# Centring ahead of the first layer and scaling by rstd after its products, for half of the tokens

## The chip, the cores and the metric

The kernel runs on one core of a Trainium2 chip. A core has a matrix engine (TensorE, "PE" in the profile), a vector engine (VectorE, DVE), a scalar engine (ScalarE, ACT), GpSimd (POOL), and SyncE (SP), which here only issues DMA transfers. Each engine runs its own list of instructions in order; they meet at semaphores. The metric is the device time of one execution in microseconds (us).

## What is computed

There are 1024 tokens of 256 features. Two layers, each behind a layer norm and added to its input; cut from the reference:

```
def _layernorm(x, axis=-1, eps=1e-05):
    m = jnp.mean(x, axis=axis, keepdims=True)
    v = jnp.var(x, axis=axis, keepdims=True)
    return (x - m) / jnp.sqrt(v + eps)
...
    # first layer: 4 experts, one per token, all three weights are the same ctx[e]
    for e in range(E):
        g = jax.nn.silu(jnp.einsum('bsd,fd->bsf', hidden_states, Wg[e]))
        u = jnp.einsum('bsd,fd->bsf', hidden_states, Wu[e])
        y = jnp.einsum('bsf,df->bsd', g * u, Wd[e])
        out = jnp.where((expert_ids == e)[..., None], y, out)
...
x = x + _L0_xattn_ref(_layernorm(x, axis=-1), itok_BxS_13_99985, ctx_2048, ctx_2048, ctx_2048)
x = x + _L0_ffn_ref(_layernorm(x, axis=-1), L0_ffn_router_w, ...)
```

In the first layer g and u use the same matrix, so the kernel computes one product z = xn ctx[e], picks for each token the one of its expert, and forms silu(z) z. The second layer has 16 routed experts of width 96 (4 per token) and a shared one. Because (x - m) ctx[e] rstd is the same as ((x - m) rstd) ctx[e], the scale by rstd, a number for each token, can be put before or after the product.

## The kernel before

Features lie on partitions (two blocks of 128, k = 0 and 1) and tokens along the rows, in two halves (h) of 512. A float32 value is split into a high part in the matrix engine's format (`_hi`) and the rest (`_lo`), and a product takes three matmuls: hi·hi, hi·lo and lo·hi.

**The norm.** x arrives by DMA with tokens on partitions, in tiles of 128 tokens; half 0 is tiles 0 to 3. DVE takes statistics of each tile (`tile_stats`, `layer_norm_vars`), POOL raises the variance to the power -0.5 (`rstd_of`), DVE makes `shift` = -mean rstd, and then DVE (tiles 0 and 2, by `BY_VECTOR`) and ACT (tiles 1 and 3) write the normed tile `xn` (`layer_norm_apply`, `apply_norm`). For half 0 this is done in two pairs of tiles. PE turns each `xn` tile with two transposes (`norm_transposes`) into banks 4 and 5; ACT copies them to `xn_hi` (`x_high`), DVE subtracts to get `xn_lo` (`x_low`).

**The mixes.** The first layer is eight calls `mix(n)`: mixes 0 and 1 are the first product of half 0 (output features 0 to 127 and 128 to 255), 2 and 3 those of half 1, 4 to 7 the second product. A mix has 4 experts with 6 matmuls of 128x512 each. The product of each expert goes into the next bank of a ring of six (banks 0 to 3, 6, 7). ACT copies expert 0 to `prod` (`first_z`), DVE copies experts 1 to 3 over it where a mask `beyond` says so (`pick`). ACT makes the silu (`silu_z`), DVE the product and its two parts (`hidden_1`), which mixes 4 to 7 read. A bank is free for PE again when its copy is done (`wait_ring_read`). Half 1's transposes stand inside mix 1, behind its expert 1.

**Weights.** They come in 15 pieces through 4 stage slots. For each, ACT writes the high part (`high_part`) and POOL the low part (`low_part`); pieces 0 to 3 are the experts' ctx matrices. SP issues all transfers in one hand-written order on one queue, and piece n waits until the parts of piece n - 4 are made.

**Before the first data.** PE runs 20 matmuls on a zeroed tile (`WARM_UP`), writing bank 7, then waits for the identity matrix (`consts_in`) and the first `xn` tile. The second layer's matmuls stand behind mix 7; the order on PE is fixed from start to end.

Of the kernel before, what the change touches and what calls it, by code (L numbers as in the profile page):

```python
# [19 lines left out]
F32 = mybir.dt.float32  # L20
# [4 lines left out]
ALU = mybir.AluOpType  # L25
# [25 lines left out]
WARM_UP = 20  # L51
# [11 lines left out]
SPREADS = 4  # L63
RING = HALVES * KC
# [14 lines left out]
def build(nc, x_d, xt_d, ids_d, ctx_d, bias_d, gu_d, wd0_d, wd_d, consts_d, out_d):  # L79
# [4 lines left out]
    with ExitStack() as ctx:  # L84
# [7 lines left out]
        x = sb("x", [P, HALVES * TT, D])  # L92
# [17 lines left out]
        shift = sb("shift", [P, NORMS, TT])  # L110
        power = sb("power", [P, TT])
# [42 lines left out]
        ids_in, xt_in, bias_in, consts_in = sem("ids_in"), sem("xt_in"), sem("bias_in"), sem("consts_in")  # L154
# [6 lines left out]
        dstep = sem("dstep")  # L161
# [22 lines left out]
        side_order = [("n1", 0, 0, 4), ("n1", 0, 1, 5), ("n1", 1, 0, 4), ("n1", 1, 1, 5),  # L184
# [12 lines left out]
        def wait_side_read(eng, b, n):  # L197
# [5 lines left out]
            if what in ("n1", "n2"):  # L203
                count = (HALVES * KC if what == "n2" else 0) + h * KC + k + 1
                eng.wait_ge(xhi_done, count)
                eng.wait_ge(xlo_done, count)
            elif what == "x1":
# [142 lines left out]
        def _(sp):  # L350
# [14 lines left out]
            sp.dma_start(x[:, TT:], x_d[:, TT:]).then_inc(x_in[2], 16)  # L365
            sp.dma_start(ids[:], ids_d.partition_broadcast(P)).then_inc(ids_in, 16)
            sp.dma_start(xt[:], xt_d).then_inc(xt_in, 16)
# [39 lines left out]
        def _(pool):  # L407
# [36 lines left out]
            rstd_of(2, 4)  # L444
            low_part(early_pieces)
            low_part(early_pieces + 1)
            rstd_of(3, 5)
# [4 lines left out]
        def _(act):  # L452
# [19 lines left out]
            def apply_norm(n, tiles=range(TT)):  # L472

                act.wait_ge(shifted, n + 2 if n > 0 or tiles[0] > 0 else 1)
                if n > 0:
                    what, hh = [("n1", 0), ("n1", 1), ("n2", 0)][n - 1]
                    act.wait_ge(side_done, side_at[what, hh, 1] + 1)
                for t in tiles:
# [4 lines left out]
            def silu_z(n):  # L483
                act.wait_ge(z_picked, (n + 1) * (E1 - 1))
# [68 lines left out]
            x_high("n1", 1, 0)  # L553
            x_high("n1", 1, 1)
            silu_z(1)
# [41 lines left out]
        def _(dve):  # L597
# [15 lines left out]
            def layer_norm_vars(n, tiles=range(TT)):  # L613
# [5 lines left out]
                s = slice(tiles[0], tiles[-1] + 1)  # L619
                nc.vector.tensor_scalar(vareps[:, n, s], meanvar[:, n, s, 1], EPS, None, ALU.add).then_inc(varied, 1)  # L620

            def layer_norm_apply(n, tiles=range(TT)):

                dve.wait_ge(powered, n + 2 if n > 0 or tiles[0] > 0 else 1)
                s = slice(tiles[0], tiles[-1] + 1)
                nc.vector.scalar_tensor_tensor(out=shift[:, n, s], in0=meanvar[:, n, s, 0], scalar=-1.0, in1=rstd[:, n, s],
                                               op0=ALU.mult, op1=ALU.mult).then_inc(shifted, 1)
                if n > 0:

                    what, hh = [("n1", 0), ("n1", 1), ("n2", 0)][n - 1]  # L630
                    dve.wait_ge(side_done, side_at[what, hh, 1] + 1)
                for t in tiles:
# [4 lines left out]
            def x_low(what, h, k):  # L637
                n = (HALVES * KC if what == "n2" else 0) + h * KC + k
                dve.wait_ge(xhi_done, n + 1)
# [187 lines left out]
            for n, tiles in enumerate((range(TT // 2), range(TT // 2, TT))):  # L827
                dve.wait_ge(x_in[n], 16)
                for t in tiles:
                    tile_stats(0, t)  # L830
                layer_norm_vars(0, tiles)
            for n, tiles in enumerate((range(TT // 2), range(TT // 2, TT))):
                layer_norm_apply(0, tiles)
            x_low("n1", 0, 0)
            x_low("n1", 0, 1)
            dve.wait_ge(x_in[2], 16)
# [304 lines left out]
```

## Time and profile before

| | us |
|---|---|
| median of 3 runs | 175.72 |
| lowest, highest | 175.63, 175.94 |
| the profiled execution | 175.69 |
| its span in the profile | 173.6 |

The page gives for this execution, over the span of 173.6 us: PE busy 168.2, DVE 117.6, ACT 68.1, POOL 40.3. The span begins when the engines start and ends with their last instruction; 2.1 us of the execution's time lie outside it. A busy time counts overlapping instructions once, and says nothing on whether anyone waits for them: for this the chain of waits and the order of time are read.

### The profile page before, as it was taken

To read this page: it belongs to the slowest core of one execution; us is meant where nothing else is said; L and a number is where in the kernel's file an instruction comes from. 1 tells how busy PE (TensorE), PEld (TensorE's weight loads), DVE (VectorE), ACT (ScalarE), POOL (GpSimd) and SP (SyncE) were. 2 spreads that over 40 slices of the span, in tenths; PEclk is the share of its full clock that TensorE was granted. 3 is DMA by queue.
4 is the path that set the end of the run, shared out by engine and by line. 5 is a ranking of instruction groups with operands and counts; after the bars stand their busy time and mean duration, and the time that the engine had idled before them with its cause. 6 is when DMAs were issued, how large, how long until landed. Compare 5 with 4: busy or idle time off the path is not lost.

```text
span 173.6 us, 2253 instructions
## 1 busy us (share of the span) xinstructions
PE 168.2 (97%) x738; PEld 131.9 (76%) x738; DVE 117.6 (68%) x267; ACT 68.1 (39%) x108; POOL 40.3 (23%) x41
## 2 busy tenths in 40 slices
PE   6989999999999999999999999999999999999992
PEld 2558888888888878888888788888878888878881
DVE  0779897885588697787688649995874544444452
ACT  2462431343115965724654582222332222222320
POOL 5593011674220006439385000000000000000000
PEclk9999999999999999999999999999999999999999
DMA  4999004065400006951111100004454221100003
GB/s 139 283 414 337 11 0 123 0 178 184 121 0 4 0 4 144 265 144 62 60 60 60 60 0 4 0 0 125 125 194 140 81 66 65 66 5 0 0 0 121
DMA packets 7451, 15.82 MB, mean 91 GB/s; under 512 B 1296, under 2 KB 1904, under 8 KB 7312
## 3 DMA queue, kind: packets, MB, share of 16 engines
q1 hardware_dynamic: 7440, 15.68, 28.5%
q8 instruction: 6, 0.10, 0.2%
q14 instruction: 5, 0.04, 0.1%
HBM read 14.56 MB, written 1.11 MB: 90 GB/s over the span
## 4 chain that ended last, share of the span: by engine, by line
PE 89%; DVE 3%; ACT 3%; DMA 2%; issue 1%; DVEq 0%; ACTq 0%
PE bank L955 24%; PE bank L1038 13%; PE bank L1037 13%; PE bank L1036 13%; PE bank L1056 7%; PE bank L1059 7%; PE bank L1057 7%; DMA x<-x_d 2%; PE bank L917 2%; PE bank L933 1%; DVE stats L611 1%; PE bank L1033 1%; PE bank L1032 1%; ACT L490 1%; ACT xn L480 1%
## 5 line engine op out<-in xcount | busy, mean ns | idle before, releaser
L1038 PE MATMUL bank<-xn_lo,gu_hi 128*128 128x512 f32 (+1 forms) x104 | 41.1, 395 | 0.0
L1036 PE MATMUL bank<-xn_hi,gu_lo 128*128 128x512 f32 x96 | 38.1, 397 | 0.0
L1037 PE MATMUL bank<-xn_hi,gu_hi 128*128 128x512 f32 x96 | 38.0, 395 | 0.0
L538 ACT ACTIVATE h_hi<-hid 128x512 fp32r<-128x512 f32 (+1 forms) x26 | 16.4, 632 | 44.4 <-DVE hid L813 44.4
L818 DVE TENSOR_TENSOR h_lo<-hid,h_hi 128x512 fp32r<-128x512 f32 (+1 forms) x26 | 21.6, 830 | 14.1 <-ACT h_hi L538 14.0
L1038 PEld LDWEIGHTS bank<-xn_lo,gu_hi 128*128 128x128 f32 (+1 forms) x104 | 19.4, 187 | 4.9
L528 ACT ACTIVATE act_sb<-bank 128x512 f32<-128x512 f32 (+1 forms) x26 | 15.4, 592 | 16.7 <-PE bank L1038 16.6
L423 POOL TENSOR_TENSOR gu_lo<-stage,gu_hi 128x512 fp32r<-128x512 f32 x12 | 16.8, 1417 | 21.4 <-ACT gu_hi L456 21.3
L1037 PEld LDWEIGHTS bank<-xn_hi,gu_hi 128*128 128x128 f32 x96 | 18.0, 188 | 4.3
L1036 PEld LDWEIGHTS bank<-xn_hi,gu_lo 128*128 128x128 f32 x96 | 18.0, 188 | 4.2
L662 DVE COPY_PREDICATED prod<-beyond,bank 128x512 f32<-128x512 uint8 x24 | 17.8, 740 | 4.9 <-PE bank L955 3.8
L1056 PE MATMUL bank<-h_hi,wd_lo 128*128 128x512 f32 (+1 forms) x52 | 20.8, 399 | 0.0
L1059 PE MATMUL bank<-h_lo,wd_hi 128*128 128x512 f32 (+1 forms) x52 | 20.6, 395 | 0.0
L1057 PE MATMUL bank<-h_hi,wd_hi 128*128 128x512 f32 (+1 forms) x52 | 20.6, 395 | 0.0
L813 DVE TENSOR_TENSOR hid<-prod,bank 128x512 f32<-128x512 f32 x24 | 16.5, 687 | 1.7
L800 DVE TENSOR_TENSOR prod<-act_sb,ids 128x512 f32<-128x512 f32 x10 | 7.6, 764 | 10.2 <-ACT act_sb L528 8.9
L800 DVE TENSOR_TENSOR prod<-act_sb,x 128x512 f32<-128x512 f32 x12 | 9.3, 778 | 7.1 <-ACT act_sb L528 7.1
L955 PE MATMUL bank<-xn_hi,ctx_hi 128*128 128x512 f32 x32 | 12.8, 400 | 0.7 <-ACT xn_hi L463 0.7
L955 PE MATMUL bank<-h_hi,ctx_hi 128*128 128x512 f32 x32 | 12.9, 403 | 0.0
L955 PE MATMUL bank<-xn_lo,ctx_hi 128*128 128x512 f32 x32 | 12.8, 399 | 0.0
L955 PE MATMUL bank<-xn_hi,ctx_lo 128*128 128x512 f32 x32 | 12.7, 396 | 0.0
L955 PE MATMUL bank<-h_lo,ctx_hi 128*128 128x512 f32 x32 | 12.7, 395 | 0.0
(104 smaller groups left out, 224.1 us busy)
## 6 DMA issues: line engine op xcount, KB each, us to landing
stage<-gu_d SPq DMA_DIRECT2D x6, 512.0 KB, 3.5
stage<-wd_d SPq DMA_DIRECT2D x3, 512.0 KB, 5.1
x<-comb_d SPq DMA_DIRECT2D x8, 192.0 KB, 2.8
ids<-comb_d SPq DMA_DIRECT2D x7, 192.0 KB, 2.7
stage<-ctx_d SPq DMA_DIRECT2D x4, 256.0 KB, 5.3
xt<-xt_d SPq DMA_DIRECT2D x1, 1024.0 KB, 9.5
x<-comb_d SPq DMA_DIRECT2D x8, 128.0 KB, 2.8
ids<-comb_d SPq DMA_DIRECT2D x6, 128.0 KB, 3.3
```

The costliest lines, as they stand in the source:

```text
L423: ins = nc.gpsimd.tensor_tensor(lo[:, s], st[:, s], hi[:, s].bitcast(F32), ALU.subtract)
L662: nc.vector.copy_predicated(prod[:, n % 2], beyond[:, e - 1, h * HALF:(h + 1) * HALF], ring_bank("z", n, e)[:]).then_inc(z_picked, 1)
L800: nc.vector.tensor_tensor(prod[:, g % 2], act_sb[:, g % 2], rows, ALU.mult).then_inc(prod_done, 1)
L813: nc.vector.tensor_tensor(hid[0:w, g % 2], src, up_bank(g)[0:w, :], ALU.mult).then_inc(hid_done, 1)
L818: nc.vector.tensor_tensor(h_lo[0:w, slot[g]], hid[0:w, g % 2], h_hi[0:w, slot[g]].bitcast(F32), ALU.subtract).then_inc(hlo_done, 1)
L955: return nc.tensor.matmul(ring_bank("z", n, e)[:], (ctx_hi, ctx_lo)[a][:, e, k, f], parts[k][b], start=start, stop=stop)
L1036: nc.tensor.matmul(out[:], gu_lo[:, cols], xn_hi[:, h, k], start=(k == 0), stop=False)
L1037: nc.tensor.matmul(out[:], gu_hi[:, cols], xn_hi[:, h, k], start=False, stop=False)
L1038: ins = nc.tensor.matmul(out[0:rows, :], gu_hi[:, wide], xn_lo[:, h, k], start=False, stop=(k == KC - 1))
L1056: nc.tensor.matmul(acc[k][:], wd_lo[0:w, c, cols], hi, start=(c == 0), stop=False)
L1057: nc.tensor.matmul(acc[k][:], wd_hi[0:w, c, cols], hi, start=False, stop=False)
L1059: ins = nc.tensor.matmul(acc[k][:], wd_hi[0:w, c, cols], lo, start=False, stop=(c == ITEMS - 1))
```

## The change

Half 0 is only centred before its products: `xn` becomes x - mean, with no rstd. `centre(t)` does this tile by tile: DVE takes mean and difference of tiles 0 and 2; ACT, by itself, of tiles 1 and 3, with a sum over the row (`accum_out` of a copy scaled by -1/256) and a second pass that adds it. The variances of half 0 are still needed: DVE takes the missing statistics of tiles 1 and 3 afterwards, POOL computes `rstd_of(0)` after the four low parts of ctx, PE turns its 128x4 numbers into 4 rows behind mix 0 (`rstd_transpose`), ACT copies them, SP writes them to DRAM and reads them back to all 128 partitions (`rstd_all`, which lies in the still unused end of `wd_lo`), and DVE multiplies `prod` of mixes 0 and 1 by them (`scale`), behind the picks and ahead of silu. Half 1 and the second layer's norms are as before.

Around this: the identity and x tiles 0 and 1 come in one transfer of 324 KB (`first_d`) in the place of 256 KB and a later one of 68 KB; DVE makes `xn_hi` of k = 1 of half 0 in ACT's place; the first mix waits for both `xn_hi` blocks and takes its six matmuls for each expert in the order hi·hi twice, lo·hi twice, hi·lo twice; there are 8 matmuls of 512 columns ahead and 8 of 256 columns between and behind the transposes in the place of 20 of 512; on DVE `hidden_1` of mixes 0 and 1 and the masks of half 1 stand later; on SP the transfers of xt, bias and pieces 4 and up stand behind the waits for the rstd rows.

```diff
-WARM_UP = 20
+WARM_UP = 8
...
-        side_order = [("n1", 0, 0, 4), ("n1", 0, 1, 5), ("n1", 1, 0, 4), ("n1", 1, 1, 5),
+        side_order = [("n1", 0, 0, 4), ("n1", 0, 1, 5), ("rstd", 0, 0, 4), ("n1", 1, 0, 4), ("n1", 1, 1, 5),
...
-            sp.dma_start(x[:, 0:TT // 2], x_d[:, 0:TT // 2]).then_inc(x_in[0], 16)
-            sp.dma_start(x[:, TT // 2:TT], x_d[:, TT // 2:TT]).then_inc(x_in[1], 16)
+            sp.dma_start(first[:, 0:FIRST + PAIR], first_d).then_inc(x_in[0], 16)
+            sp.dma_start(first[:, FIRST + PAIR:FIRST + 2 * PAIR], x_d[:, 0:PAIR]).then_inc(x_in[1], 16)
             load_piece(0)
-            sp.dma_start(consts_sb[:], consts_d).then_inc(consts_in, 16)
...
             sp.dma_start(ids[:], ids_d.partition_broadcast(P)).then_inc(ids_in, 16)
+            sp.wait_ge(rstd_turned, 1)
+            sp.dma_start(rstd_d, rstd_rows[:]).then_inc(rstd_out, 16)
+            sp.wait_ge(rstd_out, 16)
+            sp.dma_start(rstd_all, rstd_d.rearrange("t c -> (t c)").partition_broadcast(P)).then_inc(rstd_in, 16)
             sp.dma_start(xt[:], xt_d).then_inc(xt_in, 16)
...
-            rstd_of(0, 1, slice(0, TT // 2))
-            rstd_of(0, 2, slice(TT // 2, TT))
             for n in range(E1):
                 low_part(n)
-            rstd_of(1, 3)
-            pool.wait_ge(consts_in, 16)
+            rstd_of(0)
+            rstd_of(1)
+            pool.wait_ge(x_in[0], 16)
...
+            def centre(t):
+
+                act.wait_ge(x_in[t // (TT // 2)], 16)
+                nc.scalar.activation(xn[:, t], x[:, t], ACT.Copy, scale=-1.0 / D,
+                                     accum_out=minus_mean[:, t:t + 1]).then_inc(astep, 1)
+                act.wait_ge(astep, t // 2 + 1)
+                nc.scalar.activation(xn[:, t], x[:, t], ACT.Identity, bias=minus_mean[:, t:t + 1]).then_inc(normed_a, 1)
+
+            def turn_rstd():
+
+                act.wait_ge(side_done, side_at["rstd", 0, 0] + 1)
+                nc.scalar.activation(rstd_rows[:], side_bank("rstd", 0, 0)[0:TT, 0:P], ACT.Copy).then_inc(rstd_turned, 1)
...
             def silu_z(n):
-                act.wait_ge(z_picked, (n + 1) * (E1 - 1))
+                if mixes[n][1] == 0:
+                    act.wait_ge(z_scaled, n + 1)
+                else:
+                    act.wait_ge(z_picked, (n + 1) * (E1 - 1))
...
-            apply_norm(0, range(TT // 2))
+            centre(1)
+            centre(3)
             high_part(0)
-            apply_norm(0, range(TT // 2, TT))
+            x_high("n1", 0, 0)
             high_part(1)
-            x_high("n1", 0, 0)
-            x_high("n1", 0, 1)
             high_part(2)
             high_part(3)
             first_z(0)
+            turn_rstd()
             apply_norm(1)
-            silu_z(0)
             first_z(1)
             x_high("n1", 1, 0)
             x_high("n1", 1, 1)
+            silu_z(0)
             silu_z(1)
...
+            def centre(t):
+
+                dve.wait_ge(x_in[t // (TT // 2)], 16)
+                tile_stats(0, t)
+                dve.wait_ge(dstep, steps[0])
+                step(nc.vector.bn_aggr(meanvar[:, 0, t], stats[:, t]))
+                dve.wait_ge(dstep, steps[0])
+                nc.vector.tensor_scalar(xn[:, t], x[:, t], meanvar[:, 0, t, 0:1], None, ALU.subtract).then_inc(normed_v, 1)
+
+            def scale(n):
+
+                dve.wait_ge(rstd_in, 16)
+                dve.wait_ge(z_picked, (n + 1) * (E1 - 1))
+                nc.vector.tensor_tensor(prod[:, n % 2], prod[:, n % 2], rstd_all, ALU.mult).then_inc(z_scaled, 1)
...
+            centre(0)
+            centre(2)
+            dve.wait_ge(side_done, side_at["n1", 0, 1] + 1)
+            nc.vector.tensor_scalar(xn_hi[:, 0, 1], side_bank("n1", 0, 1)[:], 1.0, None, ALU.mult).then_inc(xhi_done, 1)
             x_low("n1", 0, 0)
             x_low("n1", 0, 1)
+            tile_stats(0, 1)
+            tile_stats(0, 3)
+            layer_norm_vars(0, (1, 3))
...
             pick(0, masked[0], [2, 3])
-            hidden_1(0)
             x_low("n1", 1, 0)
             x_low("n1", 1, 1)
+            scale(0)
             pick(1, masked[0])
+            scale(1)
+            hidden_1(0)
+            hidden_1(1)
             masked.append(thresholds(1))
-            hidden_1(1)
             pick(2, masked[1])
...
+                    if n == 0:
+                        for k in range(KC):
+                            operands(k, False)
+                            term(e, k, 0, 0, start=(k == 0))
+                        for k in range(KC):
+                            operands(k, True)
+                            term(e, k, 0, 1)
+                        pe.wait_ge(w_lo, e + 1)
+                        for k in range(KC):
+                            ins = term(e, k, 1, 0, stop=(k == KC - 1))
...
-            for _ in range(WARM_UP):
-                nc.tensor.matmul(bank[7][:], warm[:, 0:P], warm[:], start=True, stop=True)
-            pe.wait_ge(consts_in, 16)
-            norm_transposes("n1", 0, 0)
+            keep_warm(WARM_UP)
+            pe.wait_ge(x_in[0], 16)
+            norm_transposes("n1", 0, 0, (0, 2, 2, 1))
+            keep_warm(3, HALF // 2)
             mix(0)
+            rstd_transpose()
```

On PE, at the start of the program before (`bank` is a PSUM bank; in brackets the semaphores waited for):

```order
L1068 MATMUL bank<-warm 128x512 [waits warm_set]
L1068 MATMUL bank<-warm 128x512 x19
L917 MATMUL bank<-consts_sb,xn 128x128 [waits normed_v,consts_in]
L917 MATMUL bank<-consts_sb,xn 128x128
L917 MATMUL bank<-consts_sb,xn 128x128 [waits normed_a]
...
L955 MATMUL bank<-xn_hi,ctx_hi 128x512 [waits xhi_done,w_hi]
L955 MATMUL bank<-xn_hi,ctx_lo 128x512 [waits w_lo]
L955 MATMUL bank<-xn_lo,ctx_hi 128x512 [waits xlo_done]
```

The same place after:

```order
L953 MATMUL bank<-warm 128x512 x7
L963 MATMUL bank<-first,xn 128x128 [waits normed_v,x_in0]
L963 MATMUL bank<-first,xn 128x128
L953 MATMUL bank<-warm 128x256 x2
L963 MATMUL bank<-first,xn 128x128 [waits normed_a]
...
L953 MATMUL bank<-warm 128x256 x3
L1007 MATMUL bank<-xn_hi,ctx_hi 128x512 [waits xhi_done,w_hi]
L1007 MATMUL bank<-xn_hi,ctx_hi 128x512 [waits xhi_done]
L1007 MATMUL bank<-xn_lo,ctx_hi 128x512 [waits xlo_done] x2
L1007 MATMUL bank<-xn_hi,ctx_lo 128x512 [waits w_lo]
```

The zero matmuls are fewer and stand between the transposes, and in the first mix the matmul that needs POOL's low part of the weights went from second to fifth place.

On DVE, from the picks of mix 0 on, before:

```order
L634 TENSOR_SCALAR xn<-x,meanvar,rstd 128x256 x2
L662 COPY_PREDICATED prod<-beyond,bank 128x512 x2
L670 TENSOR_TENSOR hid<-act_sb,prod 128x512
L672 TENSOR_SCALAR h_hi<-hid 128x512
L674 TENSOR_TENSOR h_lo<-hid,h_hi 128x512
L641 TENSOR_TENSOR xn_lo<-bank,xn_hi 128x512 x2
L662 COPY_PREDICATED prod<-beyond,bank 128x512 x3
L648 TENSOR_SCALAR beyond<-ids 128x512 x3
```

and after:

```order
L679 TENSOR_TENSOR xn_lo<-bank,xn_hi 128x512 [waits side_done,xhi_done] x2
L661 TENSOR_TENSOR prod<-prod,wd_lo 128x512 [waits z_picked,rstd_in]
L700 COPY_PREDICATED prod<-beyond,bank 128x512 [waits z_done,dstep,z_first]
L700 COPY_PREDICATED prod<-beyond,bank 128x512 [waits z_picked,z_done] x2
L661 TENSOR_TENSOR prod<-prod,wd_lo 128x512 [waits z_picked,rstd_in]
L708 TENSOR_TENSOR hid<-act_sb,prod 128x512 [waits z_silu]
L710 TENSOR_SCALAR h_hi<-hid 128x512 [waits dstep]
L712 TENSOR_TENSOR h_lo<-hid,h_hi 128x512 [waits h1_high]
```

Two multiplications by the rstd rows (`wd_lo` is where they lie) came in, the first of them waits for a transfer, and the hidden values of mix 0 are made after the picks of mix 1 where they were made before them.

On SP, the queue of transfers after, from the tokens' ids on; before, the row of xt follows the row of ids at once:

```order
L375 DMA ids<-ids_d 128x1024
L377 DMA rstd_d<-rstd_rows 4x128 [waits rstd_turned]
L379 DMA wd_lo<-rstd_d 128x512 [waits rstd_out]
L380 DMA xt<-xt_d 128x2048
L381 DMA bias<-bias_d 128x16
L367 DMA stage<-gu_d 128x448 [waits w_lo,w_hi]
```

Two transfers and two waits came in, and xt, bias and all pieces from the fifth on are queued behind them.

## Rows read from the trace of the kernel before

**Rows 1.** The page: busy time and share by engine; TensorE's granted clock; chain.

```profile
PE 168.2 (97%) x738; PEld 131.9 (76%) x738; DVE 117.6 (68%) x267; ACT 68.1 (39%) x108; POOL 40.3 (23%) x41
PEclk9999999999999999999999999999999999999999
PE 89%; DVE 3%; ACT 3%; DMA 2%; issue 1%; DVEq 0%; ACTq 0%
```

**Rows 2.** The chain that ended last: start us, duration us, what.

```profile
0.74 3.59 DMA x<-x_d
4.35 0.77 DVE stats L611 x2
5.14 0.26 DVE meanvar L617 x2
...
6.83 0.60 ACT xn L480
...
7.95 0.56 ACT xn L480
...
9.03 0.51 ACT xn_hi L463
9.67 8.84 PE bank L955 x36
18.50 0.87 PE bank L917 x8
19.38 28.00 PE bank L955 x120
```

**Rows 3.** The waits of PE: who for whom, us in total, times, longest.

```profile
PE bank L955 <- ACT xn_hi L463: 0.7, 1, 0.7
```

**Rows 4.** Order of time, PE and its weight loads: start us, us, instruction.

```profile
1.31 6.78 PE L1068 MATMUL bank<-warm 128*128 128x512 bf16 x20 [1.31 <-POOL warm L408]
...
5.56 0.15 PEld L1068 LDWEIGHTS bank<-warm 128*128 128x128 bf16 x1 [0.28 <-issue]
...
5.98 1.62 PEld L1068 LDWEIGHTS bank<-warm 128*128 128x128 bf16 x8 [0.27 <-issue]
...
11.34 0.40 PE L955 MATMUL bank<-xn_hi,ctx_hi 128*128 128x512 f32 x1
```

**Rows 5.** Order of time on DVE.

```profile
6.71 0.41 DVE L634 TENSOR_SCALAR xn<-x,meanvar,rstd 128x256 f32<-128x256 f32 x1
...
9.55 1.29 DVE L641 TENSOR_TENSOR xn_lo<-bank,xn_hi 128x512 fp32r<-128x512 f32 x2 [1.36 <-ACT xn_hi L463]
...
17.90 0.69 DVE L670 TENSOR_TENSOR hid<-act_sb,prod 128x512 f32<-128x512 f32 x1 [0.70 <-ACT act_sb L487]
...
21.14 2.42 DVE L662 COPY_PREDICATED prod<-beyond,bank 128x512 f32<-128x512 uint8 x3
...
25.63 1.53 DVE L674 TENSOR_TENSOR h_lo<-hid,h_hi 128x512 fp32r<-128x512 f32 x1
27.08 2.40 DVE L662 COPY_PREDICATED prod<-beyond,bank 128x512 f32<-128x512 uint8 x3
```

**Rows 6.** Order of time on POOL, up to the rstd of half 1.

```profile
8.03 5.12 POOL L419 TENSOR_TENSOR ctx_lo<-stage,ctx_hi 128x512 fp32r<-128x512 f32 x4 [0.35 <-ACT ctx_hi L456]
...
13.25 1.11 POOL L429 TENSOR_TENSOR rstd<-vareps,power 128x4 f32<-128x4 f32 x1
```

**Rows 7.** DMA issues: count, KB each, median us to landing.

```profile
x<-x_d SPq DMA_DIRECT2D x2, 256.0 KB, 3.8
...
comb_d<-comb_row SPq DMA_DIRECT2D x2, 32.0 KB, 1.6
```

**Rows 8.** Stretch 3.00 to 4.35: busy by engine, PEclk, DMA share, GB/s.

```profile
3.00:4.35 1.35, 1.35 (x5) 0.52 (x4) 0.00 (x0) 0.00 (x0) 0.00 (x0) 1.00 0.85 254
```

**Rows 9.** Transfers to and from comb_d, 46 of them, all stages.

```profile
DMA to landing us min/median/max: 1.5/2.8/5.3
```

**Rows 10.** A small ACT instruction of the second layer.

```profile
58.71 0.26 ACT L495 ACTIVATE scores<-logit 128x64 f32<-128x64 f32 x1
```

More of the change, by code:

```diff
@@ L63 @@
 SPREADS = 4
+FIRST = P + GROUPS
+PAIR = TT // 2 * D
 RING = HALVES * KC
@@ L203, in wait_side_read @@
             if what in ("n1", "n2"):
-                count = (HALVES * KC if what == "n2" else 0) + h * KC + k + 1
+                count = (HALVES * KC if what == "n2" else 0) + h * KC + (KC if what == "n1" and h == 0 else k + 1)
                 eng.wait_ge(xhi_done, count)
                 eng.wait_ge(xlo_done, count)
+            elif what == "rstd":
+                eng.wait_ge(rstd_turned, 1)
             elif what == "x1":
@@ L470, in first_z, with apply_norm @@
                 nc.scalar.activation(prod[:, n % 2], ring_bank("z", n, 0)[:], ACT.Copy).then_inc(z_first, 1)
[L472 to L478, printed above, removed]
+            def centre(t):
[7 more added lines that the diff above has]
+                nc.scalar.activation(rstd_rows[:], side_bank("rstd", 0, 0)[0:TT, 0:P], ACT.Copy).then_inc(rstd_turned, 1)
+            def apply_norm(n):
+                act.wait_ge(shifted, n)
+                what, hh = [("n1", 0), ("n1", 1), ("n2", 0)][n - 1]
+                act.wait_ge(side_done, side_at[what, hh, 1] + 1)
+                for t in range(TT):
                     if t not in BY_VECTOR[n]:
@@ L618, in layer_norm_vars, with layer_norm_apply @@
                 dve.wait_ge(dstep, steps[0])
[L619 to L626, printed above, removed]
+                nc.vector.tensor_scalar(vareps[:, n], meanvar[:, n, :, 1], EPS, None, ALU.add).then_inc(varied, 1)
+            def centre(t):
[9 more added lines that the diff above has]
+                nc.vector.tensor_tensor(prod[:, n % 2], prod[:, n % 2], rstd_all, ALU.mult).then_inc(z_scaled, 1)
+            def layer_norm_apply(n):
+                dve.wait_ge(powered, n + 1)
+                nc.vector.scalar_tensor_tensor(out=shift[:, n], in0=meanvar[:, n, :, 0], scalar=-1.0, in1=rstd[:, n],
                                                op0=ALU.mult, op1=ALU.mult).then_inc(shifted, 1)
[L628 to L632, printed above, removed]
+                what, hh = [("n1", 0), ("n1", 1), ("n2", 0)][n - 1]
+                dve.wait_ge(side_done, side_at[what, hh, 1] + 1)
+                for t in range(TT):
                     if t in BY_VECTOR[n]:
@@ L909, in side_wait, with keep_warm, norm_transposes @@
                 return bank[b]
-            def norm_transposes(what, n, h):
+            def keep_warm(count, cols=HALF):
+                for _ in range(count):
+                    nc.tensor.matmul(bank[7][:, 0:cols], warm[:, 0:P], warm[:, 0:cols], start=True, stop=True)
+            def norm_transposes(what, n, h, between=()):
                 banks = [side_wait(what, h, k) for k in range(KC)]
                 for t in range(TT):
+                    if between:
+                        keep_warm(between[t], HALF // 2)
                     wait_normed(pe, n, t)
@@ L920, in norm_transposes, with rstd_transpose @@
                             ins.then_inc(side_done, 1)
+            def rstd_transpose():
+                pe.wait_ge(powered, 1)
+                b = side_wait("rstd", 0, 0)
+                nc.tensor.transpose(b[0:TT, 0:P], rstd[:, 0], consts_sb[:, 0:P]).then_inc(side_done, 1)
             def x1_transposes(h, pair):
@@ L961, in mix @@
                     wait_ring_read(pe, "z", n, e)
-                    for k in range(KC):
+                    if n == 0:
[8 more added lines that the diff above has]
+                            ins = term(e, k, 1, 0, stop=(k == KC - 1))
+                    for k in range(KC if n else 0):
                         if e == 0:
```

46 lines of the change are left out of this document (22 added, 24 removed).

## The prediction

> **What bounds the kernel now.** I read the page first: PE is busy 97% of the span and makes 89% of the chain that ended last [rows 1]. Then the chain in order of time: it enters PE at 9.67 and stays there but for the transposes that PE makes itself, 36 matmuls, 8 transposes in 0.87, and 120 matmuls in 28.00, which is 0.2333 us for a matmul of 512 columns [rows 2]. The waits of PE have one item worth speaking of once the data are there, 0.7 us until the first `xn_hi` [rows 3]. So from 9.67 on PE is a full queue, and the kernel's time is the moment at which mix 0 starts, plus work of fixed length, plus a tail. What comes ahead of 9.67 is a path through other engines: x lands at 4.33, DVE takes statistics (0.77 for two tiles, 0.26 for two aggregates), POOL and DVE make rstd and shift, ACT writes its first tile at 6.83 and its last at 7.95 to 8.51, PE transposes, and ACT copies `xn_hi` from 9.03 [rows 2]. The change works on this path and pays in the stretch behind it.
>
> A second reading is TensorE's clock. The weight load of the zero matmul at 5.56 and the next ones at 5.98, 8 of them in 1.62, give 0.42 us for a matmul of 512 columns and then 0.20 [rows 4]: the 1.2 GHz level first, then 2.4 GHz, after PE had worked without a break since 1.31. The granted clock of the page reads full even ahead of this, 1.00 from 3.00 to 4.35 [rows 8], so at the start the pitch is the witness.
>
> **Ahead of mix 0.** (1) The first transfer has 68 KB more. At 254 GB/s, what moved just before x landed [rows 8], this is 0.27 us; between nothing (the 68 KB of constants were already in the early traffic) and 0.4 I take 0.2, so data at 4.55. (2) DVE: statistics 0.38, one aggregate 0.13, the difference 0.41 [rows 2, 5], with small gaps 1.0 a tile, so tile 0 at 5.55 and tile 2 at 6.55. (3) ACT: two passes a tile. The trace has no ACT pass with a sum. Its nearest row is the pass with scale and bias, 0.56 to 0.60 [rows 2]; the sum may cost nothing more, or another small instruction of 0.26 [rows 10], so a tile costs 1.1 to 1.5 and two 2.2 to 3.0. Nearest is the plain pass, since it is the same engine, data and size; with a little for the wait between the two I take 2.45, so tile 3 is there at 7.0, where the last tile of before was there at 8.51. (4) PE's transposes of tiles 0 to 2 lie under this wait; the last two take 0.2 and a latency, and the copy of DVE can start at 7.4. ACT first has `high_part(0)`, 0.6, and so starts at 7.6; its copy of 512 columns takes 0.6, and `xn_hi` is complete at 8.2. DVE's half costs about 0.65, the mean of its two passes from PSUM in 1.29 [rows 5], and ends at 8.05. Mix 0 starts at 8.25, against 9.67: 1.4 earlier.
>
> (5) Not all of this is kept. `xn_lo` comes after, two subtractions in 1.29 [rows 5], ready at 8.9 and 9.55. The new order puts two hi·hi matmuls ahead (8.25 to 8.72), then waits for each `xn_lo`; the last four matmuls run from about 9.37, the last three of them from 9.6, and expert 0 ends at 10.3. Before, expert 1 started at 11.34 [rows 4]. So 1.04 earlier. POOL's low part of ctx 0, four in 5.12 or 1.28 each [rows 6], starts at 7.7 where it was 8.03 and is ready at 9.0, ahead of the fifth matmul; the others are ready by 12.8, each ahead of its expert. Nothing else is new for mix 0, whose other 18 matmuls are 4.2 us; it ends at 14.5.
>
> **Behind mix 0.** (6) One more transpose, 0.87 for 8 [rows 2] and so 0.11, with the change of operands 0.13. It waits for rstd of half 0, which POOL makes behind the low parts: 12.8 and 1.11 [rows 6], 13.95. PE comes at 14.5, so the wait is hidden with 0.5 to spare. Half 1's rstd is ready at 15.0, where it was 14.36; DVE's and ACT's tiles of half 1 are then done by 16.2, and PE wants them at 17.4.
>
> (7) The rows' way: ACT's copy of 4x128, 0.26 [rows 10], at 15.0; SP's write, 1.6, the nearest being 32 KB to DRAM [rows 7]; the broadcast of 256 KB, between the median 2.8 of smaller broadcasts [rows 9] and the 3.8 of x at a crowded start [rows 7]; I take 3.2 since the queue is empty then. The rows are there at about 19.9. DVE reaches `scale(0)` at 20.4, behind `xn_lo` of half 1, whose transposes end at 18.5. The waiting instruction would hold up the picks of mix 1, and these the ring.
>
> (8) DVE's work until it serves mix 2: two scales, 0.69 each as the product at 17.90 [rows 5], between that and 1.53, what a two-input pass took at 25.63 [rows 5] while POOL worked; POOL has nothing to do then, so 0.69. In order: scale 21.1, picks of mix 1 (three in 2.42 [rows 5]) 23.6, scale 24.3, `hidden_1` twice (1.9 each from the rows of 0.69, 0.43, 0.69) 28.1, masks 29.15, the first pick of mix 2 at 29.9. PE needs this bank for expert 3 of mix 3. With PE at 21.3 for the start of mix 2, that is at 31.1. Before, this pick stood at 27.08 [rows 5]: the cover shrinks from over 3 us to 1.2, but it holds, and 0.8 of port trouble for one `h_lo` would still fit. Later picks have 1.8 and more. Pieces 4 to 7 of the weights, put off on SP from 9.4 to about 17, land by 22, and ACT converts the first at 26.
>
> The sum: -1.04 + 0.13 = -0.9 us, on PE's full queue, which nothing further gives back. The profiled execution was 175.69 with a span of 173.6, and the median is 175.72, the same for this purpose. I predict **174.8 us**, and for this case alone 174.4 to 175.2.
>
> **The rivals.** A, the path is shorter by less. If the first data land at 4.95 (all 0.4 for the larger transfer) and each sum of ACT costs the 0.26, tile 3 is there at 7.95, mix 0 starts at about 9.0 and expert 0 ends at 10.95: -0.4 + 0.13, so 175.4, no change that can be told. For it speaks that no row shows such a pass; against, that DVE's half stays under ACT's.
>
> B, slower: the clock. PE is no longer busy without a break. Eight matmuls at 0.42 end at 4.7, the first tile comes at 5.55, and the small groups fill perhaps two thirds of the time up to 8.25. If the level is still 1.2 GHz when mix 0 starts, a matmul costs 0.467 in place of 0.233. Expert 0 then ends at 11.05 in place of 10.3, and every further matmul costs 0.233 more; the gain of 0.9 is spent when the clock rises later than 11.4. Before, it rose after 4.7 us of unbroken work [rows 4]; counted from 8.25 this is 12.95, that is four matmuls beyond expert 0, a loss of 0.75 and 0.95: 176.5. A rise by 9.3 would cost almost nothing, since mix 0 waits for `xn_lo` anyhow. For it: the rows show a rise only behind dense work. Against: much of the work stays, and 8 of 256 columns are put where the gaps are. The Trainium skill's page TensorE: Matmul & The Clock Gate, section "Part 1: The HAM clock gate", states that the low level is the default and that activity releases it, at a point that depends on where in a free-running cycle of the monitor the work starts; the rise at 5.98 agrees, and by it single executions could differ from each other here.
>
> C, the ring. If the rows land later than 21.6 in place of 19.9, that is if the two transfers take over 6.5 us together, PE waits in mix 3. With the write at 1.6 and a broadcast of 5.3, the longest of its kind [rows 9], they take 6.9 and PE loses 0.4, with one pass slowed by POOL up to 1.2: 175.2 to 176.0.
>
> D, the split is no gain because PE waits for POOL's rstd at the new transpose. It has 0.5 to spare; a POOL pass of the early pieces that is 1 us later costs 0.5: 175.3.
>
> **How the numbers follow.** The forecast 0.50, A 0.17, B 0.18, C 0.08, D 0.07. A measurement of this kernel tells about 0.2%, 0.35 us, from no change, so faster is below 175.37 and slower above 176.07. Faster: the forecast, and a third of A, C and D each: 0.61. Slower: most of B and a part of C: 0.20. The same: 0.19. The range reaches down to 174.3 (data at once, no cost of the sum) and up to 176.1, which leaves out most of B.
>
> **What would show it.** Right: the first matmul of mix 0 near 8.25, expert 1 near 10.3, the 128x256 passes of ACT with the sum near 0.6, the pitch 0.23 from the first matmul of mix 0, the end of the second transfer of rstd near 19.9 and no wait of DVE for it over 0.3, PE's waits between mix 0 and the end near nothing. Wrong: a pitch of 0.47 in mix 0 (B), a wait of PE in mix 3 for a DVE pick (C), a wait at the new transpose (D), or tile 3 at 7.5 or later (A).

## The result and the profile after

The forecast was 174.8 us. Measured, the changed kernel takes **179.26 us** (177.78 to 179.74, 4 runs) against 175.75 (175.63 to 175.94): a ratio of 1.0184, 95% interval 1.0137 to 1.0232. It is slower by 3.5 us, and the interval lies wholly above 1. The profiled execution took 179.47 with a span of 177.3.

The page, in the order of [rows 1]: busy time, TensorE's granted clock in 40 slices, chain.

```profile
PE 168.6 (95%) x735; PEld 132.1 (74%) x735; DVE 122.1 (69%) x267; ACT 69.1 (39%) x112; POOL 40.2 (23%) x40
PEclk9999999999969999999999999999999999999999
PE 51%; DVE 19%; issue 5%; ACT 4%; DMA 3%; DVEq 0%; SPq 0%; ACTq 0%
```

PE has as much work as before, but it holds 51% of the chain in the place of 89%, and DVE has 19% in the place of 3%. These shares are only a hint, since the chain goes through DVE in two places: up to 48.9, ahead of a wait of PE of 2.5 us, and again in the second layer up to 130.4, ahead of one of 0.4. One slice of the clock, the twelfth (about 49 to 53 us), is low. The waits of PE, which had one item in [rows 3]:

```profile
PE bank L985 <- DVE xt L720: 2.5, 1, 2.5
PE bank L1007 <- DVE xn_hi L868: 0.5, 1, 0.5
PE bank L1116 <- DVE xt L863: 0.4, 1, 0.4
PE bank L1007 <- DVE prod L700: 0.3, 1, 0.3
```

L985 are the transposes of x1 (half 0 after the first layer), L720 is DVE's addition of mix 5 to xt. PE's order of time, start and duration:

```profile
6.48 0.49 PE L953 MATMUL bank<-warm 128*128 128x256 bf16 x3
7.52 0.70 PE L1007 MATMUL bank<-xn_hi,ctx_hi 128*128 128x512 f32 x2 [0.55 <-DVE xn_hi L868]
...
13.91 0.48 PE L1007 MATMUL bank<-xn_hi,ctx_hi 128*128 128x512 f32 x1
...
30.04 0.40 PE L1007 MATMUL bank<-xn_lo,ctx_hi 128*128 128x512 f32 x1
30.76 0.50 PE L1007 MATMUL bank<-xn_hi,ctx_hi 128*128 128x512 f32 x1 [0.33 <-DVE prod L700]
...
46.03 0.40 PE L1007 MATMUL bank<-h_lo,ctx_hi 128*128 128x512 f32 x1
48.89 1.55 PE L985 MATMUL bank<-first,xt 128*128 128x128 f32 x8 [2.47 <-DVE xt L720]
...
51.09 0.63 PE L1007 MATMUL bank<-h_lo,ctx_hi 128*128 128x512 f32 x1
51.52 0.63 PE L1007 MATMUL bank<-h_hi,ctx_hi 128*128 128x512 f32 x1
...
55.60 1.04 PE L963 MATMUL bank<-first,xn 128*128 128x128 f32 x8
```

The chain at the same place, first before, then after:

```profile
47.37 0.87 PE bank L933 x8
48.25 4.19 PE bank L955 x18
```

```profile
48.89 1.55 PE bank L985 x8
50.44 5.33 PE bank L1007 x18
```

From these rows, and the same places of before, the gain shrinks and turns into a loss (us):

| place on PE | before | after | difference |
|---|---|---|---|
| mix 0 starts | 9.67 | 7.52 | -2.15 |
| mix 1 starts | 15.54 | 13.91 | -1.63 |
| mix 3's third expert has its last matmul's slot over | 31.81 | 30.27 | -1.54 |
| mix 6's second expert is done | 47.21 | 46.26 | -0.95 |
| transposes of x1 start (chain) | 47.37 | 48.89 | +1.52 |
| norm transposes of the second layer (chain) | 52.44 | 55.77 | +3.33 |
| span | 173.6 | 177.3 | +3.7 |

So the gain at the start is there, and larger than forecast; 0.5 goes in mix 3, 2.5 to 2.6 in one wait, and 1.8 behind it: 8 transposes take 1.55 in the chain where they took 0.87, and 18 matmuls 5.33 where they took 4.19. Of this 1.8, some 0.2 is not the clock's: behind a wait and at full clock the 8 transposes took 1.09, in the versions below with only the masks or only the cast moved. That leaves 1.6 for the clock. The last 0.4 is the wait in the second layer at 130.4. DVE there had waited for a transfer for 1.73, where it was 1.31 before; two other traces have 0.2 of such a wait and the rest none, and its cause was not tried. The windows of after show the level, 1.2 GHz at a granted clock of 0.50; by their means it was low from about 49.4 to 52.8 (columns: stretch, its length, PE's busy time with its operations, granted clock, DMA share, GB/s):

```profile
48.00:50.00 2.00, 1.11 (x7) 0.85 0.32 129
50.00:52.00 2.00, 2.00 (x8) 0.50 0.00 0
52.00:54.00 2.00, 2.00 (x9) 0.80 0.00 0
```

And DVE, up to the addition that PE waited for:

```profile
18.39 1.29 DVE L679 TENSOR_TENSOR xn_lo<-bank,xn_hi 128x512 fp32r<-128x512 f32 x2 [1.21 <-ACT xn_hi L475]
20.51 0.69 DVE L661 TENSOR_TENSOR prod<-prod,wd_lo 128x512 f32<-128x512 f32 x1 [0.83 <-DMA wd_lo<-rstd_d]
...
27.83 2.05 DVE L686 TENSOR_SCALAR beyond<-ids 128x512 uint8<-128x512 int32 x3
29.98 2.41 DVE L700 COPY_PREDICATED prod<-beyond,bank 128x512 f32<-128x512 uint8 x3
...
42.82 1.74 DVE L720 TENSOR_TENSOR xt<-prod,xt 128x512 f32<-128x512 f32 x1
44.48 1.27 DVE L728 CAST gu_hi<-gu_lo 128x32 fp32r<-128x32 f32 x1
45.66 0.72 DVE L700 COPY_PREDICATED prod<-beyond,bank 128x512 f32<-128x512 uint8 x1
```

DVE starts the picks of mix 2 at 29.98, where it was 27.08 [rows 5]. From the end of mix 0's picks (17.2 in both) that is 2.9 more, made of 1.2 for two scales, 0.9 for the wait for the rows (start to start), 1.1 for the masks, 0.4 for a longer idle ahead of `xn_lo`, 0.2 for the picks, less 0.9 for `hidden_1`, which ran beside POOL before. From 40.26 to 45.66 it loses another 2.1 against the same three steps before (37.35 to about 40.7): the first addition takes 1.74 for 0.69, and the cast of 32 columns 1.27 for 0.17. POOL works at the same time:

```profile
39.82 2.94 POOL L436 TENSOR_TENSOR wd_lo<-stage,wd_hi 128x512 fp32r<-128x512 f32 x2
42.72 2.99 POOL L436 TENSOR_TENSOR gu_lo<-stage,gu_hi 128x512 fp32r<-128x512 f32 x2
```

The lateness is 5.0 us at the picks of mix 5. In the kernel before, the same place on DVE was:

```profile
40.50 0.17 DVE L690 CAST gu_hi<-gu_lo 128x32 fp32r<-128x32 f32 x1
41.91 0.75 DVE L662 COPY_PREDICATED prod<-beyond,bank 128x512 f32<-128x512 uint8 x1 [1.23 <-PE bank L955]
43.21 0.75 DVE L662 COPY_PREDICATED prod<-beyond,bank 128x512 f32<-128x512 uint8 x1 [0.55 <-PE bank L955]
44.61 0.74 DVE L662 COPY_PREDICATED prod<-beyond,bank 128x512 f32<-128x512 uint8 x1 [0.65 <-PE bank L955]
45.45 0.69 DVE L682 TENSOR_TENSOR xt<-prod,xt 128x512 f32<-128x512 f32 x1
```

DVE waited for PE at each pick (1.23, 0.55 and 0.65) and was done at 46.14, 1.07 ahead of PE at 47.21, a slack of 3.5 in all; with PE 0.95 earlier, 5.0 - 3.5 + 0.95 is 2.45, the wait of 2.47.

### The profile page after: what moved, and what is told of

It is laid out like the page before. It is cut to its first block, busy times and chain, and to the rows that moved or that the text cites. A ratio compares the mean times of both kernels' runs of the same rounds, so it can differ in the third digit from the quotient of the medians.

```text
span 177.3 us, 2257 instructions
## 1 busy us (share of the span) xinstructions
PE 168.6 (95%) x735; PEld 132.1 (74%) x735; DVE 122.1 (69%) x267; ACT 69.1 (39%) x112; POOL 40.2 (23%) x40
## 4 chain that ended last, share of the span: by engine, by line
PE 51%; DVE 19%; issue 5%; ACT 4%; DMA 3%; DVEq 0%; SPq 0%; ACTq 0%
PE bank L1098 9%; PE bank L1096 9%; PE bank L1097 9%; PE bank L1116 5%; PE bank L1119 5%; PE bank L1117 5%; DVE prod L700 5%; PE bank L1007 4%; DVE hid L851 2%; DVE prod L838 2%; DMA ids<-comb_d 2%; DVE marked_l L763 1%; PE bank L985 1%; ACT L517 1%; PE bank L963 1%
## 5 line engine op out<-in xcount | busy, mean ns | idle before, releaser
L856 DVE TENSOR_TENSOR h_lo<-hid,h_hi 128x512 fp32r<-128x512 f32 (+1 forms) x26 | 21.6, 830 | 14.1 <-ACT h_hi L565 14.0
L436 POOL TENSOR_TENSOR gu_lo<-stage,gu_hi 128x512 fp32r<-128x512 f32 x12 | 17.2, 1453 | 21.5 <-ACT gu_hi L468 21.4
L838 DVE TENSOR_TENSOR prod<-act_sb,first 128x512 f32<-128x512 f32 x12 | 9.3, 777 | 7.0 <-ACT act_sb L555 7.0
L1007 PE MATMUL bank<-h_hi,ctx_hi 128*128 128x512 f32 x32 | 13.4, 420 | 0.0
L1007 PE MATMUL bank<-xn_hi,ctx_hi 128*128 128x512 f32 x32 | 12.3, 406 | 0.9 <-DVE xn_hi L868 0.5
L1007 PE MATMUL bank<-h_hi,ctx_lo 128*128 128x512 f32 x32 | 13.1, 410 | 0.0
```

The lines of the kernel that those rows point to most:

```text
L436: ins = nc.gpsimd.tensor_tensor(lo[:, s], st[:, s], hi[:, s].bitcast(F32), ALU.subtract)
L838: nc.vector.tensor_tensor(prod[:, g % 2], act_sb[:, g % 2], rows, ALU.mult).then_inc(prod_done, 1)
L856: nc.vector.tensor_tensor(h_lo[0:w, slot[g]], hid[0:w, g % 2], h_hi[0:w, slot[g]].bitcast(F32), ALU.subtract).then_inc(hlo_done, 1)
L1007: return nc.tensor.matmul(ring_bank("z", n, e)[:], (ctx_hi, ctx_lo)[a][:, e, k, f], parts[k][b], start=start, stop=stop)
```

## The experiments

**Theory 1:** DVE is late for the x1 transposes, because of new work, moved work and collisions with POOL; the idle time of PE there lowers the clock, which costs more still. The rivals put the price in only one of these, or take the clock for an effect of the thinner start. Kernels "of the change" start from the changed kernel, the delays from the kernel before.

### Masks and cast moved on DVE

```diff
             pick(0, masked[0], [2, 3])
+            masked.append(thresholds(1))
             x_low("n1", 1, 0)
...
             hidden_1(1)
-            masked.append(thresholds(1))
...
                 add_block_1(n)
-                if n == 4:
-                    router_low_rows()
+            router_low_rows()
             pick(6, masked[1], [1])
```

> The changed kernel with two pieces of DVE's work moved: the masks of half 1 (2.05 us at 27.83 there) go into DVE's idle time behind the picks of mix 0 (17.2 to 18.4), and the small cast of the router's low rows (1.27 us at 44.48) goes behind the second addition to xt. Theory 1, DVE is late for the transposes of x1: DVE is 3.3 us earlier there, the wait of 2.5 us of PE and the wait of 0.3 in mix 3 are gone, the clock does not fall, and the gain of 1.6 at the start of mix 1 is kept: 174.1 us. Rival, the lateness is that of the new multiplications and their transfer alone, and moved work does not matter: no faster than 177.5. Rival, the clock falls for another reason than this wait: 175.9.

Measured 174.78 us, ratio to before 0.9942 (0.9919 to 0.9965). It is faster than before, though by 1.0 and not 1.6. The masks take 1.08 in their new place, the cast 0.17. The first addition still takes 1.74, and DVE waits 1.18 for the rows; PE still waits 0.3 at the transposes of x1, and its clock reads 1.00. Another part of the difference from the 174.1 expected is at the start of the profiled execution: mix 0 began at 8.38, since the clock rose later (below); it is the slowest of the six. Two orders on DVE, with no work taken away, are worth 4.5 us.

### Ten zero matmuls in PE's wait

```diff
-            mix(6, {1: lambda: (x1_transposes(0, 0), x1_transposes(0, 1))})
+            mix(6, {1: lambda: (keep_warm(10, HALF, 4), x1_transposes(0, 0), x1_transposes(0, 1))})
```

(Bank 4 is unused there.)

> The changed kernel with ten zero matmuls of 512 columns (2.1 us) ahead of the transposes of x1, where PE waits 2.5 us. The wait for DVE stays, PE idles 0.4 at most. Theory 1, the clock falls because of this idle time and costs 1.8 us by itself (8 transposes in 1.55 for 0.87, 18 matmuls in 5.33 for 4.19): 177.5 us, with a narrow spread between executions. Rival, the fall has another cause: about 179.3, with slow matmuls behind the transposes still.

Measured 177.83 (177.68 to 178.81), mean clock 1.00 in all four runs, where the changed kernel has 0.988 to 0.990 in three and 0.997 in the fourth, its fastest at 177.78. The wait for DVE is still there behind the zero matmuls, and what follows is at full speed:

```profile
46.77 2.10 PE L953 MATMUL bank<-warm 128*128 128x512 bf16 x9
49.17 1.09 PE L985 MATMUL bank<-first,xt 128*128 128x128 f32 x8 [0.30 <-DVE xt L720]
50.02 0.48 PE L1007 MATMUL bank<-h_hi,ctx_hi 128*128 128x512 f32 x1
50.34 0.39 PE L1007 MATMUL bank<-h_hi,ctx_lo 128*128 128x512 f32 x1
```

So of the 3.5 us, some 1.4 are the clock's and 2.1 are what DVE's lateness costs net of the gain at the start. The intervals of the two kernels just touch, but the same comes from the four runs of the changed kernel (177.78 at 0.997 against 179.06 to 179.74, 1.3 to 2.0) and from the 1.6 of its trace.

### No scale by rstd

```diff
-            turn_rstd()
...
-            scale(0)
...
-            scale(1)
...
-            rstd_transpose()
```

and with them SP's two transfers and waits, so that SP also issues xt and the weight pieces earlier again.

> The changed kernel without the scale by rstd in half 0 (this part of the computation is left out): no transpose of rstd, no copy, no transfers, no waits on SP for them, no two multiplications; the centred start and the order of everything else stay. Theory 1 with the price in the new work: DVE is earlier by 0.61 twice and by its wait of 0.83 for the rows, 2.1 us in all, so PE waits some 0.5 us for x1 and the clock stays: 175.0 us. Rival, the price is in the moved masks and their collision with POOL: PE still waits over 1.5 us, 177 us or more.

Measured 174.09, ratio 0.9914 (0.9886 to 0.9942). It is 0.9 faster than I expected: PE has no wait at the transposes of x1 where I had 0.5. DVE is at the picks of mix 2 at 27.37; the masks still take 2.05 and the cast 1.27 beside POOL, but the first addition begins just ahead of POOL's pass (0.69, at 40.22) and x1 is ready at 45.2. So the moved work alone, with its collisions, fits under the slack. The new work nearly fits too, as the version with masks and cast moved shows, where PE waits 0.3; it is the two together that do not. The rival is out as it was put, but not the collision as such, which this kernel's first addition escaped by being early.

### Only the masks moved; only the cast moved

> Only the masks of half 1 moved into DVE's idle time, the cast of the router's rows stays between the additions. Theory 1: x1 is ready 2.05 us earlier, at 46.8, PE is there at 45.8, so it waits 1.0 and loses that: 175.1 us if the clock stays, up to 176 if it falls. Rival (moved work does not matter): above 177.5.

> The changed kernel with only the small cast of the router's low rows moved behind the second addition. Theory 1: x1 is ready 1.27 us earlier, at 47.6 in the place of 48.85, PE waits 1.3 in the place of 2.5 and the clock stays at its high level as in the run with the masks moved: 176.6 us. Rival, a cast of 32 columns is too small to matter: 179 us.

Masks: 176.03, ratio 1.000 (0.998 to 1.002). PE waits 1.3 for x1 in the trace and the clock stays. I had 175.1 to 176, from an x1 that is ready at 46.8; it was ready at 47.65. In this trace the new transpose was late, at 14.43, since POOL's rstd was there only at 14.37, and the broadcast took 5.2. Cast: 176.61, ratio 1.0031 (1.001 to 1.0053), as expected; PE waits 1.3 and 0.4 in mix 3. An operation on 32 columns, moved by one place, takes 2.65 us off the changed kernel's 179.26: 1.3 by not standing beside POOL ahead of the addition, and the rest, 1.4, is what the fall of the clock had cost; none of the ten runs shows it.

### The transfers on SP

On top of the masks and cast moved:

```diff
+            sp.dma_start(xt[:], xt_d).then_inc(xt_in, 16)
+            sp.dma_start(bias[:], bias_d.partition_broadcast(P)).then_inc(bias_in, 16)
             sp.wait_ge(rstd_turned, 1)
...
-            sp.dma_start(xt[:], xt_d).then_inc(xt_in, 16)
-            sp.dma_start(bias[:], bias_d.partition_broadcast(P)).then_inc(bias_in, 16)
+            sp.wait_ge(rstd_in, 16)
             for n in range(SLOTS, len(pieces) - 2):
```

> The version with masks and cast moved, and on SP xt and bias issued ahead of the wait for the rstd rows, and the weight pieces behind a wait for the rows' landing, so that nothing shares the queue with the broadcast. Theory 1, with the rows' late landing as the rest of DVE's lateness: the broadcast lands in 2.9 us in the place of 4.8 to 5.9, DVE's wait of 1.2 us for it goes, x1 is ready 1.2 us earlier, and PE's last wait of 0.35 there is gone: 0.35 faster than the version without it, 0.9915 of before. Rival, the length of the broadcast is its own and not that of what follows it: no difference from the version without it, 0.994.

Measured 174.48, ratio 0.9912 (0.9883 to 0.9941): **faster than both kernels**. The broadcast, first as in the changed kernel, then as here:

```profile
wd_lo<-rstd_d SPq DMA_DIRECT2D x1, 256.0 KB, 4.8
```

```profile
wd_lo<-rstd_d SPq DMA_DIRECT2D x1, 256.0 KB, 3.1
```

It took 5.2 with the masks and cast moved and the old queue. Here DVE has no wait for it, PE has no wait for x1, and DVE waits for PE again at the picks of mix 5:

```profile
39.59 0.69 DVE L721 TENSOR_TENSOR xt<-prod,xt 128x512 f32<-128x512 f32 x1
40.20 0.74 DVE L701 COPY_PREDICATED prod<-beyond,bank 128x512 f32<-128x512 uint8 x1
41.50 0.75 DVE L701 COPY_PREDICATED prod<-beyond,bank 128x512 f32<-128x512 uint8 x1 [0.56 <-PE bank L1007]
```

The intervals of the two versions, 0.9919 to 0.9965 and 0.9883 to 0.9941, overlap. That the queue's order helps is shown by the waits in the traces; the 0.35 us that I expected of it are not shown by the times. The same change of SP alone, on the changed kernel:

> The changed kernel with only SP's order changed (xt and bias ahead of the rstd rows, the weight pieces behind their landing). Theory 1: the broadcast lands in 3.1 us in the place of 4.8, DVE's wait of 0.8 for it goes and x1 is ready at 48.0 in the place of 48.85; PE waits 1.7 there; if the clock stays, 175.7 + 0.8 + 0.4 = 176.9 us, with the clock's fall up to 178.7. Rival, this wait does not count since the masks' collision with POOL sets DVE's end: as the changed kernel, 179.3.

Measured 177.78, ratio 1.0102 (1.0071 to 1.0134), inside what theory 1 gave. DVE starts the picks of mix 2 at 29.22 in the place of 29.98 and ends the second addition at 48.05. PE waits 2.1, where I had 1.7. The four runs were 176.86 with a clock of 1.00, and 177.74 to 178.04 with 0.988 to 0.990: the clock's fall alone is worth 1.0 here.

### DVE delayed in the kernel before

```diff
             hidden_1(3)
+            for _ in range(4):
+                step(nc.vector.tensor_scalar(spare, bank[4][:], 1.0, None, ALU.mult))
+                dve.wait_ge(dstep, steps[0])
             for n in (4, 5):
```

(`spare` is the used-up x of tiles 0 and 1, the other kernel has 8 copies in place of 4, and the copies change no result.)

> The kernel before with four useless copies of 512 columns on DVE ahead of the picks of mix 4, about 0.72 us each, 2.9 in all. Theory 1 says that DVE has 3.3 us of slack against the transposes of x1 in the kernel before (picks of mix 5 could end at 43.2 and the addition at 43.9, PE comes at 47.2): no change, 175.7 to 175.9 us. Rival, any delay of DVE here costs: 1 us or more above before.

> The kernel before with eight such copies, 5.8 us. Theory 1: x1 is ready 2.5 us after PE comes for it, so PE idles 2.5 us and then its clock falls for some 3 to 4 us, which costs another 1.8: 175.7 + 2.5 + 1.8 = 180.0 us, 178.2 in executions in which the clock does not fall. Rival, the fall of the clock belongs to the changed start (fewer zero matmuls), not to the idle time: 178.2 with a narrow spread.

Four copies: 176.61, ratio 1.0057 (1.0032 to 1.0082), not the "no change" that I expected. PE waits 0.9 at the transposes of x1. The reason is in the rows between:

```profile
42.49 1.09 DVE L683 TENSOR_TENSOR xt<-prod,xt 128x512 f32<-128x512 f32 x1
43.50 1.27 DVE L691 CAST gu_hi<-gu_lo 128x32 fp32r<-128x32 f32 x1
```

POOL's two passes for piece 8 stand at 41.74 for 2.99. A delay of 2.9 pushed these two steps under them and became 4.4. Eight copies push them beyond:

```profile
46.05 0.69 DVE L683 TENSOR_TENSOR xt<-prod,xt 128x512 f32<-128x512 f32 x1
46.66 0.18 DVE L691 CAST gu_hi<-gu_lo 128x32 fp32r<-128x32 f32 x1
```

Here the delay was 5.8 and stayed so: DVE came to the two steps when POOL's passes, done at 44.9, were over. Measured 178.38, ratio 1.0131 (1.0094 to 1.0167); PE waited 0.8 in mix 5 for a bank and 1.2 at the transposes, and the clock stayed (0.996 to 1.00). I had expected one wait of 2.5 and the clock's fall; the ring cut the wait in two. So this run says nothing on the start, and I asked again with the delay behind the last pick:

```diff
                 pick(n, masked[0])
+                for _ in range(5 if n == 5 else 0):
+                    step(nc.vector.tensor_scalar(spare, bank[4][:], 1.0, None, ALU.mult))
+                    dve.wait_ge(dstep, steps[0])
                 add_block_1(n)
```

> The kernel before with five useless copies on DVE, 3.6 us, between the picks of mix 5 and the addition that the transposes of x1 wait for, so that PE has one unbroken wait of 2.5 us there and none in the ring. Theory 1, an idle time of this length makes the clock fall, whatever the start of the kernel: 175.7 + 2.5 + 1.4 to 1.8 = 179.8 us, with a mean clock of 0.99, and single executions near 178.2 where it does not fall. Rival, the fall needs the changed start or chance: 178.2 with a clock of 1.0.

Measured 179.96 (179.71 to 180.21), ratio 1.024 (1.0217 to 1.0264), mean clock 0.989 to 0.990 in all four runs:

```profile
49.36 1.97 PE L937 MATMUL bank<-consts_sb,xt 128*128 128x128 f32 x8 [2.23 <-DVE xt L683]
50.98 0.78 PE L959 MATMUL bank<-h_hi,ctx_hi 128*128 128x512 f32 x1
51.55 0.63 PE L959 MATMUL bank<-h_hi,ctx_lo 128*128 128x512 f32 x1
51.98 0.63 PE L959 MATMUL bank<-h_lo,ctx_hi 128*128 128x512 f32 x1
```

The kernel before, with its own start of 20 zero matmuls, shows the same slow stretch as soon as PE has this one idle time. The rival that lays the fall on the changed start is out.

## Why the prediction was wrong

**What bounds the kernel** was read rightly for before: PE was a full queue from the first matmul on. What I did not ask of it was how near the other engines were.

**Ahead of mix 0 (1 to 5)** the direction was right and the size too small: mix 0 started at 7.52 where I had 8.25. The first data came at 3.85, not 4.55: the larger transfer landed in 3.1 us where the smaller had taken 3.6, so my charge of 0.2 for 68 KB had the wrong sign here. Part of this is spread: in the kernel before with delays DVE began at 4.05, 4.02 and 4.12, and not at 4.35, and in the changed kernel and its versions at 3.7 to 3.9. DVE's tile took 0.95 for 1.0. ACT's took 0.95 for the 1.22 of my sum, and the term that no row had shown is this:

```profile
3.85 0.42 ACT L487 ACTIVATE xn<-first 128x256 f32<-128x256 f32 x1 [1.84 <-DMA first<-first_d]
4.17 0.19 ACT L487 ACTIVATION_READ_ACCUMULATOR xn<-first 128x1 f32 x1
4.39 0.51 ACT L490 ACTIVATE xn<-first,minus_mean 128x256 f32<-128x256 f32 x1
```

The sum costs a second instruction of 0.19, but the pass with a constant scale is shorter, 0.42, than the row with scale and bias that I took. Expert 0 ended at 9.56, 1.78 earlier than before, where I had 1.04.

**Behind mix 0 (6)** held in the sum but not in its margin: the new transpose cost 0.15 for my 0.13. Since PE was earlier than forecast, the 0.5 to spare was used up: POOL's row of rstd ends at 13.83, and the transpose starts at 13.88, 6.36 after mix 0, where it was 6.22 to 6.24 in five other traces with rstd in time. That is 0.1 of rival D at most; in the version with only the masks moved it was 0.6 (6.87).

**(7), the rows' way,** was short by the broadcast: 4.8 for 3.2. The write took less than its 1.6: SP issued it at 14.48 and the broadcast at 15.68. I took the queue as empty and overlooked that SP issues xt and the pieces right behind it; with these held back it took 3.1. The rows came near 20.5, and DVE waited 0.8.

**(8), DVE's work.** The forecast's 29.9 is the end of the first pick of mix 2, since the masks end at 29.15; the 27.08 beside it is that pick's start before, so that the two do not compare. Measured, the pick began at 29.98 and ended at 30.71, 0.8 late. DVE was free for the scale at 19.7 and not 20.4, the wait of 0.8 used this up, the steps up to the masks gave 0.3 back, and the masks took 2.05 for 1.05, beside POOL. PE was there at 30.27 and not 31.1, 0.8 early. So the cover of 1.2 became a wait of 0.5 in mix 3. It is the wait of rival C, but not by its condition: the rows landed at 20.5, ahead of its 21.6.

**The step that failed** is "Later picks have 1.8 and more", and with it, in the sum, "on PE's full queue, which nothing further gives back". I followed DVE's lateness only to those who wait for a bank of the ring. The next one to wait is `x1_transposes`, for DVE's second addition to xt, at 47.2. In the kernel before it had 1.07 in hand and 2.4 of DVE's waits ahead of it; the changed kernel brought 5.0 us of lateness to that place. Of this I had worked out 2.1 (29.15 against 27.08, start to start) and let it end there; it was 2.9, and 2.1 more arose on the way by two steps that slid under POOL passes. In the terms of the sum, my -0.9 was -1.6 at the start of mix 1, and what I had put at nothing behind it was 0.7 in mixes 1 to 6 (0.5 of it the ring), 2.5 for the wait at the transposes of x1, 1.8 right behind it, most of it the clock, and 0.4 in the second layer: +3.7 in the span. I had priced a collision once, 0.8, as port trouble of one `h_lo`, and in fact there were three, of 1.0, 1.05 and 1.1.

**Rival B** had the right mechanism at the wrong place. The clock was at its high level when mix 0 started; it fell at about 49.4, for some 3.4 us, behind PE's wait, and cost 1.4 to 1.6 us. I gave 0.18 to a fall at the start and nothing to one later, since I had no later wait. The range ended at 176.1, short of the 179.26, for the same reason: each rival was a case by itself, while here the ring, the rows' landing and the clock followed from one cause, DVE being late, and added up.

## What to carry to other kernels

When a full engine is moved ahead and another takes on work, follow the second one's lateness to every instruction that waits for it until its slack is used up or given back, and not only to the nearest ring of buffers; the slack is its idle time plus what the waiter has in hand. A late engine also slides under other engines' work: look at what stands beside each step at its new time, above all a short step that can be moved behind the one that others wait for. Work that is not needed yet belongs into an idle time of the same engine (here masks of 1.08 us, where late they cost 2.05), and a transfer that someone waits for should have nothing queued right behind it.

## What the runs showed of the hardware

**DVE beside POOL.** A cast of 32 columns took 0.17 us alone and 1.27 beside POOL's subtraction, an addition of 512 columns 0.69 and 1.74, three masks 1.08 and 2.05. These read as waiting and not as slower work. POOL's passes, taken one by one in the changed kernel, end at 28.92, 44.01 and 45.70, and the three DVE instructions counted above began beside them at 27.83, 42.82 and 44.48 and ended at 29.21, 44.55 and 45.74. Each thus ended 0.0 to 0.5 behind the pass, and the second and third mask, behind it, took 0.41 each. In the kernel without rstd DVE's addition began first, at 40.22, and kept its 0.69, while POOL's pass took 1.82 for 1.29. Not every step pays: the picks, which read a PSUM bank, took 2.45 for three fully beside POOL (at 40.26) and 2.42 alone. The Trainium skill, SBUF — State Buffer, section "Terms", says that the ports which DVE and GpSimd share are locked for a full instruction and the loser fully blocks; these rows agree for the steps that lost time.

**TensorE's clock fell behind waits of 2 us.** The lengths are those of the one profiled execution of each kernel. With 2.2 and with 2.5 us of idle time it fell in 4 of 4 and in 3 of 4 runs, with 2.1 (in the trace that kept its level) in 3 of 4, with one wait of 1.3, or with 0.8 and 1.2 five microseconds apart, in none that shows a mean below 0.996. It then ran at 1.2 GHz for 3 to 4 us, a price of 1.0 to 1.6 us. What else beside the wait decides whether it falls was not tried.

**When it rises at the start differs between executions.** With the same code ahead, the zero matmuls of 256 columns show it at 5.3 us, at 2.4 GHz in the changed kernel and at 1.2 GHz in the version with masks and cast moved, where mix 0 began at 8.38:

```profile
5.28 0.38 PE L953 MATMUL bank<-warm 128*128 128x256 bf16 x2
```

```profile
5.43 0.63 PE L952 MATMUL bank<-warm 128*128 128x256 bf16 x2
```

This is 0.9 us on the path, about the spread of each version's times. Over the changed kernel and its seven versions mix 0 began at 7.5 to 7.6 in five traces, at 7.83 in one, and at 8.38 and 8.50 in two. In the kernel before and its delayed versions the 20 zero matmuls ended between 7.2 and 8.5, and mix 0 began between 9.36 and 10.06.

**What stays open:** how the 1.0 us of the version with masks and cast moved divides between this spread and its remaining waits was not separated in the times, only in single traces; and whether the first data land earlier because of the larger transfer or by chance was not tried.
